# Item numbers beyond the table read copies of the last combined row

## What is computed

```
h = emb; acc = emb
for _ in range(2):
    h = segment_sum(adj_val[:, None] * h[adj_col], adj_row, N)
    acc = acc + h
graph = acc / 3
combined = graph[items] + item_features[items]          # items: 512 x 50
seq = take_along_axis(combined, alias_inputs[..., None], axis=1)
mask = (inputs != 0)
hs = sum(seq * mask, 1) / sum(mask, 1)
nh = tanh(concat([flip(emb[:50]), seq], -1) @ w_1)
nh = sigmoid(nh @ glu1_w.T + glu1_b + (hs @ glu2_w.T)[:, None, :])
sess = sum((nh @ w_2) * mask * seq, 1)
scores = 12 * l2norm(sess) @ l2norm(graph).T            # 512 x 12501
```

## Time and profile before

| | us |
|---|---|
| timed runs | 4176.29, 4176.44, 4177.8 |
| median | 4176.44 |
| span of the profiled execution | 6020.2 |
| first gather of layer 0 | at 756.4 |
| first gather of layer 1 | at 3262.6 |
| first gather of `combined` | at 5596.6 |
| last gather of `combined` | at 5902.3 |

### The profile page before, as it was taken

The page is one execution under the profiler, slowest core; times in us unless marked ns, Lnnn a source line. Parts: engine busy times, 40 slices in busy tenths (PEclk is TensorE's granted clock), DMA queues, the critical chain, the costliest instruction groups (busy, mean ns, idle before and its releaser), DMA issues.

```text
span 6020.2 us, 68764 instructions
## 1 busy us (share of the span) xinstructions
PE 3070.2 (51%) x9778; PEld 1849.5 (31%) x9778; DVE 3014.4 (50%) x7257; ACT 866.4 (14%) x3005; POOL 2890.1 (48%) x2965
## 2 busy tenths in 40 slices
PE   5988744444444444444444444444444444445578
PEld 3777622222222222222222222222222222222344
DVE  8999754444444444444444444444444444445455
ACT  2998800000000000000000000000000000000543
POOL 1666654444444444444445454454454454455561
PEclk8888866666666666666666666666666666666689
DMA  0000011111111111111114111111111111112454
GB/s 25 4 3 3 3 48 33 32 31 32 32 31 33 33 34 33 34 33 31 32 32 120 34 37 35 33 37 36 32 37 35 33 37 35 34 36 80 79 84 139
DMA packets 162229, 235.35 MB, mean 39 GB/s; under 512 B 67554, under 2 KB 107776, under 8 KB 161952
## 3 DMA queue, kind: packets, MB, share of 16 engines
q0 software_dynamic: 92896, 171.14, 12.4%
q1 hardware_dynamic: 54132, 58.90, 3.0%
q10 hardware_dynamic: 15052, 3.83, 0.3%
HBM read 192.69 MB, written 41.01 MB: 39 GB/s over the span
## 4 chain that ended last, share of the span: by engine, by line
ACTq 49%; issue 32%; DVE 7%; PE 6%; ACT 3%; another core or an unknown queue 2%; POOL 1%; DMA 0%; DVEq 0%; SPq 0%; POOLq 0%
ACTq L686 43%; ACTq L682 5%; ACT big L644 2%; PE bank L1520 1%; PE bank L1382 1%; POOL sorted_edges L542 1%; DVE stage L944 1%; PE bank L1548 1%; DVE acc L1167 1%; DVE big L888 1%; PE bank L1507 1%; DVE ring L896 0%; PE bank L1482 0%; DVE big L904 0%
## 5 line engine op out<-in xcount | busy, mean ns | idle before, releaser
L1444 PE MATMUL bank<-ring 128*128 128x256 f32 x4976 | 2105.7, 558 | 2135.8 <-DVE ring L1118 1194.1
L1444 PEld LDWEIGHTS bank<-ring 128*128 128x128 f32 x4976 | 1147.7, 263 | 3071.0 <-DVE ring L1118 1662.5
L574 POOL DMA_INDIRECT ring<-in_L_rec_emb,cring x1195 | 1134.9, 950 | 1336.2 <-ACT cring L662 978.9
L1167 DVE TENSOR_TENSOR acc<-acc,bank 128x256 f32 x2488 | 1029.6, 414 | 1481.3 <-remote 1131.6
L1118 DVE TENSOR_SCALAR ring<-bank,mlo,mval 128x256 f32<-128x256 f32 x2488 | 1343.5, 540 | 742.4 <-DMA ring<-in_L_rec_emb 523.1
L574 POOL DMA_INDIRECT ring<-table,cring x1195 | 1130.2, 946 | 1202.8 <-PE bank L1444 795.7
L644 ACT ACTIVATE big<-big 128x68 f32<-128x68 bf16 x1764 | 557.7, 405 | 1.2 <-issue 1.2
L1382 PE MATMUL bank<-big,ring 128*128 128x136 f32 x2352 | 430.8, 328 | 75.5 <-issue 20.8
L542 POOL DMA_INDIRECT sorted_edges<-moved,block_to x313 | 397.2, 1269 | 100.3 <-issue 100.0
L1382 PEld LDWEIGHTS bank<-big,ring 128*128 128x128 f32 x2352 | 356.8, 219 | 147.6 <-ACT big L644 83.2
L660 ACT COPY mlo<-ring 128x24 f32 (+1 forms) x104 | 21.7, 209 | 2415.0 <-issue 2381.6
(11 more groups left out here) (213 smaller groups left out, 1700.7 us busy)
## 6 DMA issues: line engine op xcount, KB each, us to landing
ring<-in_L_rec_emb SPq DMA_DIRECT2D x3136, 0.5 KB
ring<-in_L_rec_emb ACTq DMA_DIRECT2D x3136, 0.5 KB
ring<-table ACTq DMA_DIRECT2D x3136, 0.5 KB
ring<-table SPq DMA_DIRECT2D x3136, 0.5 KB
scores<-stage SPq DMA_DIRECT2D x48, 512.0 KB
ring<-in_L_rec_emb,cring POOLq DMA_INDIRECT x1195
ring<-table,cring POOLq DMA_INDIRECT x1195
table<-big SPq DMA_DIRECT2D x7, 896.0 KB, 9.1
```

What stands on the lines that cost most here:

```text
L574: pool.indirect_dma_start(msg[:, s, :], None, source, bass.IndirectOffsetOnAxis(cring[:, s:s + 1], 0)).then_inc(s_g[s], 16)
L1167: add = dve.tensor_tensor(acc[:, bass.ds(off, BUCKET)], acc[:, bass.ds(off, BUCKET)], bank[u % PR][:, 0:BUCKET], ALU.add)
L1444: pe.matmul(bank[u % PR][:, 0:BUCKET], msg[:, h * T + u, :], onehot[:, u % SR, :], start=True, stop=True).then_inc(s_mm[u % M], 1)
```

## The change

Item numbers that are N or more are sent behind the table. DVE adds FAR = 2^20 to them and clamps not to N - 1 but to a number of the partition's own, `copy_at[p]` = ROWS + 5p (ROWS = 12544), which POOL makes by an iota at the program's start. The tensor `combined` gets 640 more rows, five per partition, all filled with row 12500: PE multiplies a broadcast column of the identity with the block of `ring` that holds that row, which puts it on all 128 partitions of a bank; DVE copies it into `ring`, and SP writes it five times per partition by one more DMA. POOL and DVE wait for eight writes in place of seven. Of its five copies a partition reads the first; the result is the same. The semaphore `s_iota` is replaced by further counts of `s_row`.

```diff
-        combined = nc.dram_tensor("combined", [ROWS, D], F32).ap()
+        combined = nc.dram_tensor("combined", [ROWS + P * APART, D], F32).ap()
...
+        copies = combined[ROWS:ROWS + P * APART, :].rearrange("(p a) d -> p a d", a=APART)
...
                 sp.dma_start(tab[1][:, a:b, :], ring_rows[:, a:b, :]).then_inc(s_cw, 16)
+            sp.wait_ge(s_copy, 2)
+            sp.dma_start(copies, ring[:, ROWS:ROWS + D].unsqueeze(1).broadcast_to([P, APART, D])).then_inc(s_cw, 16)
...
+            pool.iota(copy_at[:, :], [[0, 1]], base=ROWS, channel_multiplier=APART,
+                      allow_small_or_imprecise_dtypes=True).then_inc(s_cst, 1)
...
-            pool.wait_ge(s_cw, 16 * (NB // GRP))
+            pool.wait_ge(s_cw, 16 * (NB // GRP + 1))
...
-                link(dve.tensor_scalar(it_n[:, :, :], it_f[:, :, :], 0.0, float(N - 1), ALU.max, ALU.min))
+                link(dve.tensor_scalar(it_n[:, :, :], it_f[:, :, :], float(N), FAR, ALU.is_ge, ALU.mult))
+                link(dve.tensor_tensor(it_f[:, :, :], it_f[:, :, :], it_n[:, :, :], ALU.add))
+                link(dve.tensor_scalar(it_n[:, :, :], it_f[:, :, :], 0.0, copy_at[:, 0:1], ALU.max, ALU.min))
...
             dve.wait_ge(s_cmb, NB)
+            dve.wait_ge(s_copy, 1)
+            dve.tensor_copy(ring[:, ROWS:ROWS + D], bank[4][:, 3 * P:3 * P + D]).then_inc(s_copy, 1)
...
-            dve.wait_ge(s_cw, 16 * (NB // GRP))
+            dve.wait_ge(s_cw, 16 * (NB // GRP + 1))
...
+            pe.wait_ge(s_cmb, NB)
+            row = N - 1 - P * (N // P)
+            pe.matmul(bank[4][:, 3 * P:3 * P + D], ident[:, row:row + 1].broadcast_to([P, P]),
+                      ring[:, N // P * D:(N // P + 1) * D], start=True, stop=True).then_inc(s_copy, 1)
             pe.wait_ge(s_g2r, NB)
```

More of the change, by code:

```diff
@@ L78, in recommender_program @@
     FAR = float(2 ** 20)
+    APART = 5
+    assert N + FAR + N < 2 ** 24 and (ROWS + P) <= 2 * L * D
     SR, PR, LEAD = 8, 4, 4
@@ L268, in recommender_program @@
         junkl = sb("junkl", [P, BT, L])
+        copy_at = sb("copy_at", [P, 1])
         ssq = sb("ssq", [P, 2 * NB])
@@ L339, in recommender_program @@
         s_mrdy = sem("s_mrdy")
-        s_iota = sem("s_iota")
         s_lines = sem("s_lines")
@@ L362, in recommender_program @@
         s_cw = sem("s_cw")
+        s_copy = sem("s_copy")
         s_wT = sem("s_wT")
@@ L407, in recommender_program @@
         emb_rest = N - emb_full * P
-        tab = [t.rearrange("(g p) d -> p g d", p=P) for t in (table1, combined)]
+        tab = [t[0:ROWS, :].rearrange("(g p) d -> p g d", p=P) for t in (table1, combined)]
+        copies = combined[ROWS:ROWS + P * APART, :].rearrange("(p a) d -> p a d", a=APART)
         big_rows = big[:, :].rearrange("p (g d) -> p g d", d=D)
@@ L524, in _ @@
                       allow_small_or_imprecise_dtypes=True).then_inc(s_cst, 1)
-            pool.wait_ge(s_cst, 11)
+            pool.iota(copy_at[:, :], [[0, 1]], base=ROWS, channel_multiplier=APART,
+                      allow_small_or_imprecise_dtypes=True).then_inc(s_cst, 1)
+            pool.wait_ge(s_cst, 12)
             pool.memset(block_id[0:1, 0:SKIP], FAR).then_inc(s_cst, 1)
@@ L619, in _ @@
             act.copy(posb[:, :], bank[6][:, 0:L]).then_inc(s_posc, 1)
-            act.wait_ge(s_cst, 14)
+            act.wait_ge(s_cst, 15)
             act.copy(row_p, iota_p[:, :]).then_inc(s_row, 1)
@@ L665, in _ @@
             act.activation(acc[:, :], ones[:, 0:1].broadcast_to([P, ROWS]), ACT.Copy, scale=0.0).then_inc(s_az, 1)
-            act.copy(bank[7][:, 0:BUCKET], iota_r[:, :]).then_inc(s_iota, 1)
+            act.copy(bank[7][:, 0:BUCKET], iota_r[:, :]).then_inc(s_row, 1)
             for m in range(-(-NT // P)):
@@ L837, in _ @@
             dve.wait_ge(s_red, GR)
-            dve.wait_ge(s_cst, 14)
+            dve.wait_ge(s_cst, 15)
             link(dve.tensor_scalar(gpad_i[:, :, :], gcnt[:, :, :], float(R - 1), None, ALU.add))
@@ L1179, in _ @@
             dve.wait_ge(s_az, 3)
-            dve.wait_ge(s_iota, 1)
+            dve.wait_ge(s_row, 3)
             for layer in range(LAYERS):
```

## The result

| | before, us | after, us |
|---|---|---|
| median of the timed runs | 4177.12 (4 runs, 4176.29 to 4179.16) | 4152.22 (4 runs, 4149.32 to 4155.03) |
| span of the profiled execution | 6020.2 | 4150.1 |
| ratio of the medians, 95% interval | | 0.9937 [0.9923, 0.9951] |

The changed kernel is 24.9 us faster, 0.6%. The forecast was 2 us and its range ended at 4164; the case that came in is its first rival.

The account below looks back on a forecast made before the run. GpSimd's issue was taken to bound the tail for two batch tiles, TensorE the rest. Terms of -2.8 (stages), -0.5 (tile 1's landing), +1.2 (copies) and 0 gave -2.1 off 4176.4: 4174 us, range 4164 to 4181.

Parts of the forecast that it names:

- first rival: Stages 1 and 2: the repeated row binds in timed runs; net gain 8.4 us at g = 1.47, 4160 us at 1.55; chance 0.25.
- What bounds the kernel: Tail from the first gather of `combined`: GpSimd's issue binds two batch tiles, TensorE the rest; 353.7 us.
- the lateness in stages 1 and 2: Last gather of tile 2 lands 92g - 126 late for TensorE: 2.8 us at g = 1.40, nothing at 1.35.
- g: Engine time per gather beside score writes in stages 1 and 2: 1.40 or 1.35 us before, 0.57 with spread rows.
- The 353 us are used up without it: Argument against the repeated row binding: the tail's terms sum to 353.7 us, against 353 us left of the timed run.
- The rebuilt run: Whole timed run: 756.4 us, two layers of 1494, waits of 39 and 40, then the tail; agrees with the median to 2 us.
- Late signals: Tail: VectorE takes TensorE's transposes late in the profile, a 70 us surplus; counted as nothing in timed runs.
- The packet when spread: Gathers of `combined`, each partition reading its own row: 0.25 us per packet, beside writes too.
- The copies' DMA: SP's write of 640 rows ahead of the first gather of `combined`: 1.2 us later, all of it counting.
- TensorE's broadcast and VectorE's copy: Ahead of the first gather of `combined`: VectorE loses 1.1 us, covered by 2.3 us, so no cost.
- The two instructions on the item numbers: VectorE at the start of layer 0: some 0.4 us each, hidden behind the gathers; at most 0.8 us.
- The copies don't spread: Rival for the gathers of `combined`: copies served as slowly as one row, packet 0.73 to 1.08 us, 4177.6 us; chance 0.12.

Follow-up runs that it names:

- e5_apart_1: Changed kernel with 128 copies 512 B apart in place of 640 rows, copies 2560 B apart; 4146.73 us, 0.9907 of before on its chip.
- e9_apart_1: Changed kernel with 128 copies 512 B apart, run again on another chip; 4149.21 us, 0.9929 of before.
- e9_after: The changed kernel run again with no edit, on one chip with two other variants; 4152.54 us, 0.9942 of before.

## Why the prediction was wrong

**What bounds the kernel: half right.** POOL's 1.25 us per gather up to stage 1 and TensorE after it is what after does: 133.1, 66.9, 66.1 and 84.5 us against 135, 67.0, 67.0 and 84.7, which sum to 350.6 against 353.7. As a description of before it is wrong in stages 1 and 2.

**The failed step: the lateness in stages 1 and 2, with a term too small and a term missing.** The gain there was taken as 2.8 us; stages 1 and 2 became 28.6 us shorter.

The term too small is g, the time per gather beside the score writes. The prediction took 1.40 us, from a packet of 1.08 us and 0.32 us of writes. It measured 1.53 us: a packet of 1.25 us and 0.24 us of writes, at a share of 0.98. By the prediction's own formula the last gather then lands 135 + 92 x 1.53 + 2 = 278 us after the first one starts, and it did (4074.8 - 3796.7 = 278.1). That is 92 x 1.53 - 126 = 15 us late, where 2.8 us were forecast.

The term missing is the second path, the held score buffers. The rival's working with g = 1.53 gives 4176.4 - 14.8 - 0.5 + 1.2 = 4162 us, which lies within the stated range and 10 us above the measured time. Against the model's 134 us stages 1 and 2 of before are 27.6 us too long, so that 13 us are left for this path; the 11 us by which the last gather had landed ahead of its use say the same in the trace. The split is an estimate, since both paths come from the same full engines and no run has the one without the other.

The packet's price was read from an execution in which stages 1 and 2 were stretched; that the two streams met less densely there, and that this made it 1.08 and not 1.25 us, is argued, not shown. The prediction said this of the rival and then took the stretch's number all the same. The same row held a warning: its 630 packets in 30 us are 19.7 gathers, 1.52 us each, while both streams together kept the engines 0.93 busy. The prediction added up the shares as if a gather could use all of the engines' time, and did not count the gathers that got through.

**The reason that it was believed: a sum that closed by chance.** "The 353 us are used up without it" was the main argument against the rival. The rebuilt run was 3823 + 353.7 = 4177 us, 1 us from the median. The two errors behind this are of one size:

| term | rebuilt, us | before measured, us | surplus, us |
|---|---|---|---|
| sorting, to the first gather | 756.4 | 743.1 | 13.3 |
| layer 0 with the wait behind it | 1494 + 39 | 1529.0 | 4.0 |
| layer 1 with the wait behind it | 1494 + 40 | 1524.6 | 9.4 |
| to stage 1 | 135 | 133.7 | 1.3 |
| stages 1 and 2 | 134 | 161.6 | -27.6 |
| stage 3 to the end | 84.7 | 84.3 | 0.4 |

The measured terms are from the openings above and this line (first and last start of each layer's gathers), before:

```profile
L574 POOL DMA_INDIRECT ring<-in_L_rec_emb,cring x1195: 940/944/3327, 743.1 to 2239.1; - x200
L574 POOL DMA_INDIRECT ring<-table,cring x1195: 940/944/961, 2272.1 to 3763.1; - x200
```

The head was taken at the stretched execution's 756.4, 39 and 40 us, all of them upper ends, though the layers beside them had been judged stretched. These 26.7 us hid the 27.6 us of lateness. A closure to 1 us is evidence only as good as the worst term in it, and a term of 800 us taken from an execution 44% too long was not good to 25 us.

**Late signals: right.** Neither after nor before profiled again shows them, and the 70 us that were left out belong to the odd execution alone.

**The packet when spread: right.** Taken as 0.25 us beside writes, measured 0.27 us. The share in the 34 us from the first gather fell to 0.19 (0.2 was forecast), and that of the gathers' queue beside the score writes to 21.2% (below 30%).

**The copies' DMA: right.** 1.2 us was forecast; POOL's wait ahead of the first gather is 33.8 us after and 32.6 before, 1.2 us more. Ahead of the first gather the queue is full (97% of sixteen engines before and after). With 128 rows in place of 640 (`e5_apart_1` and `e9_apart_1`) the same wait is 32.9 us, 0.3 more than before. By the prediction's price per row one engine would have shown as 18 us and eight as 2.3, so 1.2 us says sixteen. The Trainium skill (DMA: Bandwidth & Descriptors, "Why a DMA increments its semaphore by 16 and not by 1") has sixteen engines for 640 rows, and the trace agrees. The other 1.6 us by which the first gather came later lie in the layers before it, which the change touches only by the item numbers; two executions can differ by that much (after's own spans are 4150.1 and, in `e9_after`, 4144.8).

**TensorE's broadcast and VectorE's copy: right, hidden.** The copy in the timeline of VectorE after:

```profile
3789.26 0.29 DVE L1229 COPY ring<-bank 128x128 f32<-128x128 f32 x1 [0.95 <-PE bank L1491]
```

VectorE loses 0.95 + 0.29 = 1.2 us (1.1 was forecast), ten us ahead of the gathers' start.

**The two instructions on the item numbers: right, hidden.** They take 0.26 and 0.37 us beside VectorE's work in layer 0:

```profile
762.11 0.26 DVE L1136 TENSOR_SCALAR it_n<-it_f 128x200 f32<-128x200 f32 x1
762.41 0.37 DVE L1137 TENSOR_TENSOR it_f<-it_f,it_n 128x200 f32<-128x200 f32 x1
```

**The copies don't spread: fell.** They spread at a distance of 2560 B and of 512 B alike.

The corrected sum, from before's profile to after's: stages 1 and 2 -28.6, the copies' DMA +1.2, the layers +1.6, the stretch to stage 1 -0.6, the end +0.2: -26.2 us, which is 4150.1 - 4176.4 but for rounding; the medians differ by 24.9.

## What to carry to other kernels

Compare the span of a profile with the timed runs before reading anything else, and if they differ, take another profile ahead of any sum; where none is to be had, let the range take in the error of every term, however well the sum closes. A DMA packet's price read from a slack execution was too low for a dense one here: add up all streams that share the engines, count what gets through in the stretch itself, and ask what buffers the other stream holds when it lands late too. If many reads go to one row of HBM and another stream fills the rest of the engines' time, give them at least a second copy; two rows did nearly as well as 128.

## What the runs showed of the hardware that was not expected

- **One row read over and over has no fixed price.** In before, with the gathers as the only stream and 53 GB/s throughout, the gathers' queue takes 83.7% of the engines from 3840 to 3870, but 34.3% from 3915 to 3930: 1.04 and 0.44 us per packet. The windows show it as a DMA share of 0.84 and 0.35:

```profile
3840.00:3870.00 30.00, 19.75 (x62) 9.43 (x60) 10.32 (x36) 17.37 (x53) 22.69 (x25) 0.77 0.84 53
3915.00:3930.00 15.00, 10.38 (x44) 6.58 (x43) 9.89 (x36) 8.59 (x23) 11.34 (x13) 0.89 0.35 53
```

  The same stretches of after both lie at 0.20. What sets the price was not found. It is not how often the row is repeated: with the item and alias numbers that the reference draws for seed 0, the repeated row is 73.5% of the rows in the gathers of either stretch, since the alias mixes the positions.
- **The price may differ from chip to chip.** Before took 4175.5, 4176.7 and 4177.1 us in three of the comparisons and 4186.3 in the fourth, on a chip of its own. The kernels that read different rows took 4146.7 and 4149.1 there, and one of them (`e5_apart_1`) 4149.2 on another chip (`e9_apart_1`). Before was not profiled on that chip, so that its stages 1 and 2 hold the 10 us is a guess.
- **GpSimd's issue of an indirect gather took 952 ns in two kernels and 943 to 945 in the others**, worth some 18 us of 4150. Neither the number of copies nor eight bytes more in front of the tiles does it alone; the cause is open.
- **An execution of 6020 us of a kernel that takes 4176.** It was seen once, with late signals and slow issuing on ScalarE's queue; the spans of the thirteen profiles taken later all lie within 8 us of their kernel's median. Its cause is open.
